# Graph attention on one core: all value products of a graph in one step, block transposes of two heads each

## What is computed

```python
q, k, v = (split_heads(x @ W + b) for W, b in ((Wq, bq), (Wk, bk), (Wv, bv)))
scores = einsum('bhqd,bhkd->bhqk', q, k) / sqrt(32) + beta * adj
scores = where(adj > 0, scores, -9e15)
out = einsum('bhqk,bhkd->bhqd', softmax(scores), v)      # heads side by side: 384 columns
y = layernorm(x + out)
```

## Time and profile before

| What | before |
|---|---|
| median of 3 runs | 627.44 us |
| profiled execution | 627.84 us |
| its span | 626.0 us |
| PE busy | 600.2 us (96%) |
| DVE busy | 587.9 us (94%) |
| ACT busy | 578.1 us (92%) |
| POOL busy | 403.9 us (65%) |
| block transposes on DVE (L592) | 308, 196.6 us, 684 ns each |
| O matmuls (L390) | 98.1 us busy |

### The profile page before, as it was taken

How to read it: one execution, slowest core, us unless ns; L and a number is a source line. 1 busy time by engine, 2 the same in 40 slices (tenths; PEclk the granted TensorE clock), 3 DMA queues, 4 the chain that set the end, 5 groups by cost and what they waited for, 6 DMA issues and landing times. The chain is left out here.

```text
span 626.0 us, 20619 instructions
## 1 busy us (share of the span) xinstructions
PE 600.2 (96%) x6064; PEld 486.8 (78%) x6064; DVE 587.9 (94%) x2256; ACT 578.1 (92%) x2063; POOL 403.9 (65%) x641
## 2 busy tenths in 40 slices
PE   5999999999999999999999999999999999999981
PEld 5888888787878888887878788887878788887750
DVE  3799999999999999999999999999999999999784
ACT  3899999999999999999999999999999999999972
POOL 2432327667767666776766777776677677667672
PEclk9999999999999999999999999999999999999996
DMA  6239889888889988888997888898888899887722
GB/s 193 86 84 201 177 173 223 190 202 203 194 205 206 206 198 202 197 201 194 224 194 197 203 201 199 199 230 180 203 203 201 199 203 214 193 202 177 180 78 102
DMA packets 68207, 117.62 MB, mean 188 GB/s; under 512 B 10496, under 2 KB 36352, under 8 KB 68096
## 3 DMA queue, kind: packets, MB, share of 16 engines
q1 hardware_dynamic: 67008, 116.10, 80.6%
q10 hardware_dynamic: 1088, 0.20, 0.2%
HBM read 22.94 MB, written 12.58 MB: 57 GB/s over the span
## 5 line engine op out<-in xcount | busy, mean ns | idle before, releaser
L471 ACT ACTIVATE probs<-neg_scores,neg_max 128x256 f32<-128x256 f32 x768 | 382.0, 502 | 4.4 <-DVE neg_max L557 0.8
L557 DVE CUSTOM_DVE_ANT_0 neg_scores<-s_bank,bias_sb 128x256 f32<-128x256 f32 x768 | 279.8, 414 | 11.0 <-PE s_bank L437 9.6
L592 DVE STREAM_TRANSPOSE blocks<-probs 128x512 f32<-128x512 f32 x308 | 196.6, 684 | 0.0
L471 ACT ACTIVATION_READ_ACCUMULATOR probs<-neg_scores,neg_max 128x1 f32 x768 | 148.6, 194 | 0.0
L770 POOL TENSOR_SCALAR adj_sb<-adj_sb,beta_col 128x512 f32<-128x512 f32 x32 | 64.2, 2006 | 88.4 <-DVE bias_sb L605 88.4
L361 PE MATMUL j_bank<-xt_high,w_high 128*128 128x256 f32 x576 | 113.2, 305 | 1.6 <-ACT w_high L502 1.5
L437 PE MATMUL s_bank<-qk 32*128 32x256 f32 x1536 | 110.0, 400 | 4.0 <-DVE neg_max L557 3.4
L487 ACT ACTIVATE qk<-j_bank,qk_bias 128x256 f32<-128x256 f32 x192 | 90.2, 470 | 19.7 <-PE j_bank L361 19.7
L437 PEld LDWEIGHTS s_bank<-qk 32*128 32x128 f32 x1536 | 69.6, 184 | 44.0 <-ACT qk L487 13.7
L812 POOL TENSOR_SCALAR att<-att,rstd,shift 128x384 f32<-128x384 f32 x58 | 95.7, 1656 | 6.4 <-POOL shift L809 6.4
L361 PE MATMUL j_bank<-xt_high,w_low 128*128 128x256 f32 x576 | 99.6, 281 | 0.0
(11 more groups left out here) (73 smaller groups left out, 868.5 us busy)
## 6 DMA issues: line engine op xcount, KB each, us to landing
shuffled<-blocks SPq DMA_DIRECT2D x480, 160.0 KB, 4.1
x_sb<-in_x_dram SPq DMA_DIRECT2D x32, 384.0 KB, 6.1
out_dram<-att SPq DMA_DIRECT2D x31, 384.0 KB, 3.6
adj_sb<-in_adj_dram SPq DMA_DIRECT2D x32, 256.0 KB, 6.2
shuffled<-blocks SPq DMA_DIRECT2D x16, 128.0 KB, 2.8
blocks<-in_L_gnn_Wq_dram SPq DMA_DIRECT2D x1, 576.0 KB, 5.7
blocks<-in_L_gnn_Wk_dram SPq DMA_DIRECT2D x1, 576.0 KB, 9.2
blocks<-in_L_gnn_Wv_dram SPq DMA_DIRECT2D x1, 576.0 KB, 10.1
```

The source lines that it names most:

```text
L471: nc.scalar.activation(probs[:, (T * s + t) % (T * NX), :], neg_scores[:, (T * s + t) % (T * NH), :], ACT.Exp, bias=neg_max[:, n % 2, t, h ...
L557: nc.vector.tensor_tensor_reduce(neg_scores[:, (T * s + t) % (T * NH), :], s_bank[h % J][:, t * N:(t + 1) * N], bias_sb[:, n % 2, t, :], - ...
L592: nc.vector.transpose(blocks[:, n % 2, :, h, :, :].rearrange("p k t q -> p t k q"), probs[:, slot:slot + T, :].rearrange("p t (k q) -> p t ...
```

## The change

The three O jobs of a graph all stand in step 0, and G0, G1 and G2 in steps 2, 3 and 6. V0 moves from step 7 to step 5, V1 from step 11 to step 7, Q1 from step 5 to step 4. `heads_t` has three buffers, `v_sb` three in place of four, and `probs` six slots in place of five. DVE turns two heads with one instruction: heads 0 and 1, then 2 and 3 in step 3, heads 4 to 7 likewise in step 7, heads 8 and 9 in step 10. Each waits for the exponentials of its second head. In step 3, G is taken ahead of the turned heads. The counter `blocks_ready` now counts pairs.

```diff
-    NX = 5
+    NX = 6
...
-                0: (("O", 0, n - 2),),
+                0: (("O", 0, n - 2), ("O", 1, n - 2), ("O", 2, n - 2)),
                 1: (("X", 0, n + 2), ("K", 0, n + 1)),
                 2: (("G", 0, n - 2), ("Q", 0, n + 1)),
-                3: (("K", 1, n + 1),),
-                4: (("O", 1, n - 2),),
-                5: (("X", 1, n + 2), ("Q", 1, n + 1)),
-                6: (("G", 1, n - 2), ("Q", 2, n + 1)),
-                7: (("V", 0, n + 1),),
-                8: (("O", 2, n - 2),),
+                3: (("G", 1, n - 2), ("K", 1, n + 1)),
+                4: (("Q", 1, n + 1),),
+                5: (("X", 1, n + 2), ("V", 0, n + 1)),
+                6: (("G", 2, n - 2), ("Q", 2, n + 1)),
+                7: (("V", 1, n + 1),),
                 9: (("X", 2, n + 2), ("K", 2, n + 1)),
-                10: (("G", 2, n - 2),),
-                11: (("V", 1, n + 1),),
...
-    heads_slot = {job[1:]: i % 2 for i, job in enumerate([job for job in ring if job[0] == "O"])}
+    heads_slot = {job[1:]: i % 3 for i, job in enumerate([job for job in ring if job[0] == "O"])}
...
-        v_sb = sb("v_sb", [P, 4, T, D])
+        v_sb = sb("v_sb", [P, 3, T, D])
...
-        heads_t = sb("heads_t", [P, 2, N])
+        heads_t = sb("heads_t", [P, 3, N])
...
-                    wait(eng, blocks_ready, before + 1 - turned_before[before])
+                    wait(eng, blocks_ready, (before - turned_before[before]) // 2 + 1)
...
-                sp.wait_ge(blocks_ready, HV * n + heads)
+                sp.wait_ge(blocks_ready, (HV * n + heads) // 2)
...
-                dve.wait_ge(exp_ready, T * (H * n + h + 1))
+                dve.wait_ge(exp_ready, T * (H * n + h + 2))
...
-                nc.vector.transpose(blocks[:, n % 2, :, h, :, :].rearrange("p k t q -> p t k q"),
-                                    probs[:, slot:slot + T, :].rearrange("p t (k q) -> p t k q", q=HD)).then_inc(blocks_ready, 1)
+                nc.vector.transpose(blocks[:, n % 2, :, h:h + 2, :, :].rearrange("p k h t q -> p (h t) k q"),
+                                    probs[:, slot:slot + 2 * T, :].rearrange("p t (k q) -> p t k q", q=HD)).then_inc(blocks_ready, 1)
...
-                    if h % J == 0:
-                        turned_now = (h,)
-                    elif h % J == 3 and h < HV:
-                        turned_now = (h - 2, h - 1, h)
+                    if h % J == 3:
+                        for job in jobs_of(n, h):
+                            if job[0] == "G":
+                                take(job)
+
+                    if h % J == 3 and h < HV:
+                        turned_now = (h - 3, h - 1)
                     else:
-                        turned_now = range(2 * J + 1, HV) if h == 2 * J + 2 else ()
+                        turned_now = (2 * J,) if h == 2 * J + 2 else ()
```

More of the change, by code:

```diff
@@ L79, in jobs_of @@
             jobs = {
-                0: (("O", 0, n - 2),),
-                1: (("O", 1, n - 2),),
-                2: (("G", 0, n - 2), ("O", 2, n - 2)),
+                0: (("O", 0, n - 2), ("O", 1, n - 2), ("O", 2, n - 2)),
+                2: (("G", 0, n - 2),),
                 3: (("G", 1, n - 2),),
@@ L389, in values @@
                                 probs_k = probs_k.rearrange("p (t a q) -> p a t q", t=T, a=J)
-                        mm = pe.matmul(b[HD * j:HD * (j + 1), 0:N], v_sb[:, n % 4, k, h * HD:(h + 1) * HD],
+                        mm = pe.matmul(b[HD * j:HD * (j + 1), 0:N], v_sb[:, n % 3, k, h * HD:(h + 1) * HD],
                                        probs_k, start=(k == 0), stop=(k == T - 1))
@@ L488, in take @@
                 elif kind == "V":
-                    ins = nc.scalar.activation(v_sb[:, n % 4, a, :], b[:, 0:D], ACT.Identity)
+                    ins = nc.scalar.activation(v_sb[:, n % 3, a, :], b[:, 0:D], ACT.Identity)
                 elif kind == "X":
@@ L743, in _ @@
                         for job in jobs_of(n, h):
-                            if h % J != 2 or job[0] not in "TG":
+                            if job[0] not in ("", "", "TG", "G")[h % J]:
                                 take(job)
```

## The result

The changed kernel takes **643.37 us** (median of 4 runs, 643.04 to 644.21); the kernel before, on the same chip, 627.39 us. The ratio is 1.0258 [1.0245, 1.027]: slower by 16.0 us. The forecast was slower by 6.5 us, 633.9 us, with a range up to 639. The direction came out as forecast, and the two loops of waits that the prediction summed are the ones that set the pace. The size did not: one wait inside a loop was missed, and so was the lower clock at both ends of the run.

A forecast was written before the change was run, and what follows sets the result against it. PE set the old pace of 18.40 us; Chain 1, 18.54 a graph, was to take over. +3.9 for 28 passes and +2.6 for the first two gave +6.5, so 633.9 us, range 621 to 639.

The forecast's parts named there:

- the two loops of waits: Chain 1 and Chain 2 across PE, ACT and DVE, forecast at 18.54 and 18.53 us a graph.
- Pairs on DVE: Transposes on DVE: a pair costs 1.15 us; five pairs for ten single ones save 0.3 us a graph.
- What the pairs wait for: Head 6's first exponential on ACT needs heads 0 and 1 turned: its delay grows from 0.74 to 1.26 us.
- Values in one step: On PE, nine tile-shape changes a graph become seven, saving about 0.22 us; PE then needs 18.18 us.
- Chain 1: Loop from the scores of heads 4 to 7 to the next graph's, over PE, ACT, DVE: 18.54 us.
- the 28 passes: Graph 2 to graph 30 at 18.54 us, 0.14 over the old pace each: +3.9 us.
- Chain 2: Loop by the slots of probabilities, from X2 over head 6's exponentials to X2: 18.22 plus 0.31, so 18.53 us.
- The first two passes: Start of the run, not bound by PE: 18.15 us a pass, 36.3 against 33.70 for both, +2.6 us.
- The end left as it is: The last graph was taken as unchanged, with 1 us for the range.
- PE as the bound: Rival: Chain 1 is at least 0.36 us shorter, PE's 18.18 sets the pace, 621.2 us; chance 0.22.
- no change: Rival: faster PE projections and a Chain 2 0.1 us shorter keep the pace at 18.4, 627 to 628.5; chance 0.12.
- A dear pair: Rival on DVE: a pair costs more than two single transposes, say 1.5 us, giving 644 us; chance 0.04.

The follow-up runs named there:

- e5: The changed kernel with each pair turned as two one-head instructions at the same places; 643.16 us, ratio 1.0249.
- e9: e4 with V1 in step 8 in place of step 7; 629.24 us, ratio 1.0029.
- e4: The changed kernel with every head turned singly in its old step, new job order and buffers kept; 632.35 us, ratio 1.0078.
- e6: The changed kernel with Q1, V0 and V1 of the first two graphs in their old steps 5, 7 and 11; 640.51 us, ratio 1.0212.
- e11: The changed kernel with the last graph's value jobs in steps 0, 1 and 2 as before; 640.84 us, ratio 1.0206.
- e1: The changed kernel with V1 in step 8 in place of step 7; 654.53 us, ratio 1.0433.
- e2: The changed kernel with heads 8 and 9 turned singly in steps 8 and 10, other pairs kept; 631.88 us, ratio 1.0085.
- e8: e9 with the first two graphs' jobs in their old steps, as in e6; 627.93 us, ratio 1.0014.

## Why the prediction was right in direction and wrong in size

- *Pairs on DVE: right.* Pairs (0,1) and (2,3) together take 2.29 us to the next start (309.66 to 311.95), the single pair in step 10 1.17 (321.08 to 322.25); 1.15 each was taken. Four single ones in e5 take 2.40 (310.08 to 312.48), so a pair saves 0.05. e5 shows that the merging itself moves nothing.
- *What the pairs wait for: right.* Head 6 starts 1.28 us after the turning starts (309.66 to 310.94); 1.26 was worked out.
- *Values in one step: the sign right, the size not.* Without its 0.45 us of waiting PE needs 18.27 of the 18.72, and e9 runs at 18.27, where 18.18 was summed. Instead of 0.22 a graph, PE saves 0.13. The Trainium skill (TensorEngine Tiling, Key Properties) says that a change of tiling mode drains TensorE; the trace agrees, as far as the pace of e9 goes, but in the changed kernel no gain follows from it, as PE itself waits there.
- *Chain 1: the right steps, 0.18 short.* 6.13, 5.99, 2.83 and 3.77 stand against 6.06, 5.99, 2.76 and 3.73. Of the 0.18, 0.06 are head 10's wait, which belongs to the slots; with 18.66 in place of 18.54 the 28 passes would have been forecast 3.4 us dearer.
- *Chain 2: **the term that failed**.* It was summed as the old loop plus and minus edits: 9.10 on DVE, 1.26 for head 6, and 8.17 from head 6 to xt_low of X2. These are 9.02, 1.27 and 8.43. The last piece was taken as ACT working through its queue without a stop, with two copies fewer. But head 10 also takes slots, those of pair (4,5), and so the piece runs over X1, DVE and that pair: 2.34 + 0.39 + 2.05 + 1.27 + 2.38. The prediction saw that a pair holds back whoever takes its first slot and applied it to head 6 alone. Summed over both waits, the loop is 18.72, the pace measured. The 28 passes took 9.09 us more instead of 3.9: 5.2 us short.
- *The first two passes: +2.6 forecast, +5.2 measured.* From S(1) of graph 0 the first takes 18.24 (22.43 to 40.67), where 18.15 was forecast, the second 20.65 (40.67 to 61.32), 2.5 more than forecast. The longer chain was foreseen; that PE's wait would bring the clock down to 0.50 was not. That graph 2 is only 4.24 later is luck: this execution's S(1) of graph 0 came 0.95 earlier, while e4 and e6, with the same jobs up to there, show 23.12 and 23.10.
- *The end left as it is: put at nothing, 1.9 measured.* The same happens there: PE waits 2.63 us ahead of the last graph's scores at 612.14, and the granted clock is 0.80 and 0.86 in the two stretches of 5 us from 610. e11 takes that back. Together 5.2 + 2.6 + 1.9 less the 0.95 are 8.7 us, which is what lies between the 15.24 us of the two spans and the 6.5 forecast; the medians are 0.7 us further apart than the spans.
- *The rivals.* PE as the bound and no change are excluded by PE's waits and the pace of 18.72. A dear pair (644 us) would have given nearly the time measured, but the rows exclude it: 1.13 to 1.17, not 1.5. A time alone would have confirmed the wrong rival.

Chain 1 and the loop of the slots are within 0.06 us of each other, 18.66 and 18.72. e1 shows that easing chain 1 gains nothing while the slots' loop holds, e5 that easing the slots' loop gains nothing while chain 1 holds, and e2, which eases both, gets 0.30 a graph back. Either alone holds the pace above 18.6. What stays open is which of the two was the longer in each graph: the rows of one graph put the slots' loop ahead by 0.06, too little to say it for all.

## What to carry to other kernels

When instructions are merged or moved on an engine with little room, list every consumer that waits for a buffer which the merged one frees, and sum the loop over all of them, not over the first. A place in a queue can be worth more than the work in it: here PE and DVE had less work and ACT hardly more (578.1 us before, 581.2 after), the merging cost nothing, and the places of ten transposes cost 10.8 us, while one copy moved by one step cost 11 us in one kernel and gained 3 in another. Start and end of a pipeline have other jobs than the middle, and an order that is made for the middle should be tried there apart.

## What was not expected of the hardware

A wait of PE can cost more than its length. With 3.22 us of waiting, up to 40.67, the granted clock was 0.50 from 41 to 46 us; with 2.27 us, up to 596.09 (e8), it was 0.54 from 595 to 600; with the 0.90 of the earlier trace rows it stayed at 1.00. In between it goes both ways: with a wait of 2.69 us ahead of the same S(1), the profiled executions of e4 and e9 show 0.66 and 0.77 in the stretch from 41 to 46 us, that of e2 1.00. Ahead of the last graph's scores PE waits 2.28 us in these three kernels; in the stretch from 600 to 605 us e4 shows 1.00, e9 0.69 and e2 0.75. This fits the wide spread of e9's runs, 625.83 to 631.04 us at mean clocks from 0.990 to 0.982, where e8, with 0.90 us in that place, lies within 627.71 and 628.46; what decides it in one execution is not shown.
